# A batched double residual product: x of the first eight units loaded by four rows in a run and multiplied in 32x128 tiles

## The chip, the cores and the metric

One core of one Trainium2 chip. The metric is the time on the device in microseconds for one execution of the whole kernel; lower is better.

## The reference

For each of 128 batches b there is an x of 64 channels by 512 times (fp32), a number `itok_B_0_7[b]` that picks one of 8 matrices W0 (64x64), and a number `itok_B_1_198[b]` that picks one of 200 matrices W1 (64x64):

```python
def layer(x, index, weights):                 # einsum 'bct,bcd->bdt'
    return jnp.einsum('bct,bcd->bdt', x, weights[index])

x = x + layer(x, itok_B_0_7, L0_cond_weights)
x = x + layer(x, itok_B_1_198, L1_cond_weights)
return x
```

So out[b] = M[b]^T x[b] with M[b] = (I + W0[b]) (I + W1[b]), a 64x64 matrix for each batch. x is 16.78 MB, the output as much.

## The kernel before

**Tiling.** A slot is 4 batches, a unit two slots (8 batches, 1 MB of x). x of a slot lies in SBUF as 128 partitions: 4 batches times 32 pairs of rows; a partition holds 2 consecutive channels (J = 2) of 512 times, so each of the 128 pieces of a load is 4 KB (`x_view`, L70, L127). The array `xy` has a place for all 32 slots, and the output of a slot is written over its x. Stores have the same form (`out_view`, L72).

**Start.** SP loads the condition numbers, x of unit 0 and half of unit 1 (L129 to L131), waits for `s_w0b_early`, and then issues all the other loads. POOL makes the identity and issues the indirect DMA that gathers the 128 matrices W1 (L148). PE turns W0 by transposes (L171), DVE writes I + W0 to `w0t` (L349), and copies the 16 matrices of units 0 and 1 to `w0b` (L360); POOL copies those of units 2 to 15 (L163). Meanwhile ACT and PE work on dummy copies and transposes (L378, L176). When the gather has landed, DVE adds one to the diagonals of W1 (L365), PE transposes W1 four columns at a time (64 transposes, L186), and DVE and ACT take turns at copying them to `w1` (L269).

**M.** `products(k)` (L190) makes the M of a block of units, for each batch and each j a product of a 64x32 stationary slice of `w0b` and the 64x64 `w1`, 32 matmuls for two units. The blocks are unit 0, unit 1, and then pairs of units. DVE (even slots) and ACT (odd slots) copy M to `m_diag` (`copy_m`, L284, two operations of 128x256 for a block of two units), multiplied by a mask of zeros and ones, so that a 64x128 stationary tile holds the M of two batches with zeros beside them.

**Apply.** `apply(k)` (L211): a slot takes 2 (j) x 2 (half h of the partitions) matmuls of a 64x128 tile with 512 columns; the two halves are two row tiles and write to two PSUM banks. Each fp32 matmul is two instructions in the profile. Unit 0 alone goes by `apply_single` (L231): 32x64 tiles, eight of them side by side, with no zeros multiplied, and its M copied plainly (L276); its output is stored in 2 KB pieces (L312). DVE and ACT each copy half of a slot's output from PSUM (L303; L282 for unit 0), two operations of 64x512 for a slot and engine. ACT issues the stores, a unit at a time behind the first copy of the next unit, the last unit's two slots one by one (L305, L380).

**Order of the work.** PE: products(0), then for each block k products(k+1) and apply(k). PSUM: three pairs of banks for outputs (`Y_RING`), so that slot s waits for the copies of slot s-3, and one pair (banks 6, 7) for M. DVE and ACT: the copies in the order of PE's work.

Of the kernel before, what the change touches and what calls it, by code (L numbers as in the profile page):

```python
# [5 lines left out]
def bass_cond_residual_kernel(  # L6
# [23 lines left out]

    fp32 = mybir.dt.float32
    i32 = mybir.dt.int32
    ALU = mybir.AluOpType
# [4 lines left out]
    J = 2  # L38
    Q = C // J
    SLOT = 4  # L40
    SLOTS = B // SLOT
    UNIT = 2 * SLOT
    UNITS = B // UNIT
    BANK = 512
# [6 lines left out]
    M_COLUMNS = 4  # L51
    M_RING = 8

    M_BANKS = [6, 4] + [6] * 7
    Y_RING = 3
    TURN = 4
    TURNS = C // TURN
    W1_RING = 6

    EARLY = 2  # L60
# [7 lines left out]
    QUARTERS = [slice(r * Q, (r + 1) * Q) for r in range(SLOT)]  # L68

    x_view = x_dram.rearrange("(s b) (p j) t -> (b p) s (j t)", b=SLOT, j=J)  # L70
    single_out_view = out_dram.rearrange("(s r) c t -> s c r t", r=SLOT)
    out_view = out_dram.rearrange("(s b) (q i) t -> (b q) s (i t)", b=SLOT, i=J)  # L72

    ctx = ExitStack()
    with ctx:  # L75
# [6 lines left out]
        xy = sb("xy", [P, SLOTS, J * T], fp32)  # L82
        w0_rows = sb("w0_rows", [P, ROWS, C], fp32)
        w0t = sb("w0t", [P, S0 * C], fp32)
        w1_rows = sb("w1_rows", [B, C, C], fp32)
        w1 = sb("w1", [P, UNITS * SLOT, C], fp32)
        w0b = sb("w0b", [P, UNITS * SLOT, C], fp32)
        m_diag = sb("m_diag", [P, 2, M_RING, J, P], fp32)
        ident = sb("ident", [P, P], fp32)
        mask = sb("mask", [P, 2], fp32)  # L90
# [10 lines left out]
        s_mask = sem("s_mask")  # L101
# [4 lines left out]
        s_w0t = sem("s_w0t")  # L106
        s_w1_plus = sem("s_w1_plus")
# [15 lines left out]

        @block.sync
        def _(sp):
            def load(s, n):
                sp.dma_start(xy[:, s:s + n, :], x_view[:, s:s + n, :]).then_inc(s_x[s // 2], 16)  # L127

            sp.dma_start(cond[:, :], cond_dram.rearrange("(b o) -> b o", o=1)).then_inc(s_cond, 16)  # L129
            load(0, 2)  # L130
            load(2, 1)  # L131

            sp.wait_ge(s_w0b_early, EARLY * UNIT)
            load(3, 1)
            for v in range(2, UNITS):
                load(2 * v, 2)
            for v in range(UNITS):
                sp.wait_ge(s_out[v], 32 if v < SINGLE or v == UNITS - 1 else 16)

        @block.gpsimd  # L140
        def _(pool):
# [12 lines left out]
            for first in range(EARLY * UNIT, B, 2 * UNIT):  # L154
                _, picked = nc.values_load_multi_w_load_instructions(  # L155
                    subjects[0:1, first:first + 2 * UNIT], engines=(POOL,), min_val=0, max_val=S0 - 1,
                    skip_runtime_bounds_check_because="subjects index the 8 matrices")
                if first == EARLY * UNIT:
                    pool.wait_ge(s_gather, 16)
                    pool.wait_ge(s_w0t, 4)  # L160
                for n in range(2 * UNIT):
                    v, odd, r = (first + n) // UNIT, n // SLOT % 2, n % SLOT
                    nc.gpsimd.tensor_copy(w0b[HALVES[odd], v * SLOT + r, :],  # L163
                                          w0t[HALVES[odd], bass.ds(picked[n] * C, C)]).then_inc(s_w0b, 1)

        @block.tensor
        def _(pe):
# [21 lines left out]

            def products(k):  # L190

                first, n = BLOCKS[k]
                if first + n <= EARLY:
                    pe.wait_ge(s_w0b_early, UNIT * (first + n))
                else:
                    pe.wait_ge(s_w0b, UNIT * (first + n - EARLY))
                if k >= 2:

                    pe.wait_ge(s_m_v, 2 * k)
                    pe.wait_ge(s_m_s, 2 * k)  # L200
                for v in range(first, first + n):
                    for j in range(J):
                        for r in range(SLOT):
                            for odd, rows in enumerate(HALVES):
                                at = (v % M_COLUMNS * J + j) * C
                                last = nc.tensor.matmul(psum[QUARTERS[r], M_BANKS[k] + odd, at:at + C],  # L206
                                                        w0b[rows, v * SLOT + r, j * Q:(j + 1) * Q],
                                                        w1[rows, v * SLOT + r, :], start=True, stop=True)
                last.then_inc(s_m_psum, 1)

            def apply(k):  # L211

                first, n = BLOCKS[k]
                pe.wait_ge(s_m_v, 2 * (k + 1))
                pe.wait_ge(s_m_s, 2 * (k + 1))
                for s in range(2 * first, 2 * (first + n)):
                    v, odd = s // 2, s % 2
                    pe.wait_ge(s_x[v], 32 if v == 1 else 16)
                    if s >= Y_RING:

                        pe.wait_ge(s_y_v, 2 * (s - Y_RING + 1))
                        pe.wait_ge(s_y_s, 2 * (s - Y_RING + 1))
                    for j in range(J):
                        for h, rows in enumerate(HALVES):
                            last = nc.tensor.matmul(psum[:, 2 * (s % Y_RING) + h, :],  # L225
                                                    m_diag[rows, odd, v % M_RING, j, :],
                                                    xy[rows, s, j * T:(j + 1) * T],
                                                    start=j == 0, stop=j == J - 1)
                    last.then_inc(s_y_psum, 1)

            def apply_single(k):  # L231

                v = BLOCKS[k][0]
                pe.wait_ge(s_m_v, 2 * (k + 1))
                pe.wait_ge(s_m_s, 2 * (k + 1))
                pe.wait_ge(s_x[v], 32 if v == 1 else 16)
                for half in range(2):
                    s = 2 * v + half
                    if s >= Y_RING:

                        pe.wait_ge(s_y_v, 2 * (s - Y_RING + 1))
                        pe.wait_ge(s_y_s, 2 * (s - Y_RING + 1))
                    for j in range(J):
                        for h in range(2):
                            rows = QUARTERS[2 * half + h]
                            for odd, columns in enumerate(HALVES):
                                last = nc.tensor.matmul(psum[columns, 2 * (s % Y_RING) + h, :],  # L247
                                                        m_diag[rows, odd, v, j, 0:C],
                                                        xy[rows, 2 * v + odd, j * T:(j + 1) * T],
                                                        start=j == 0, stop=j == J - 1)  # L250
                    last.then_inc(s_y_psum, 1)
# [4 lines left out]
            for k in range(len(BLOCKS)):  # L256
                if k + 1 < len(BLOCKS):
                    products(k + 1)
# [149 lines left out]
```

## Time and profile before

| | |
|---|---|
| median of 3 runs | 92.74 us (92.63 to 92.84) |
| the profiled execution's own time | 92.7 us |
| its span, first to last instruction | 90.8 us |
| granted TensorE clock, mean over the span | 0.968 |
| busy: PE, DVE, ACT, POOL | 76.8, 60.0, 57.0, 23.5 us |
| DMA | 35.93 MB, mean 396 GB/s |

Times in the rows are microseconds from the start of the span. In the timelines and the chain, L12 is line 12 of the kernel, PE a matmul, PEld a weight load, "q" behind an engine its sequencer, where DMAs are issued. "x32" counts instructions.

### The profile page before, as it was taken

What the parts mean: (1) busy time and instruction counts of PE and PEld (TensorE: products, weight loads), DVE (VectorE), ACT (ScalarE), POOL (GpSimd) and SP (SyncE); (2) the same over time, 40 slices, a digit from 0 to 9 for tenths busy, and PEclk for the clock granted to TensorE, in tenths of its full rate; (3) what the DMA queues carried; (4) which work ended last, traced back from release to release, by engine and by line L of the source; (5) the groups of instructions that cost most, each with busy time, mean ns of one, the idle gap of its engine ahead of it and who ended that gap; (6) DMA issues with size and microseconds to landing.
All of it is one profiled execution on the core that took longest, in us unless ns stands there. A gap on an engine that the chain in (4) does not pass through costs nothing.

```text
span 90.8 us, 2458 instructions
## 1 busy us (share of the span) xinstructions
PE 76.8 (85%) x906; PEld 42.9 (47%) x906; DVE 60.0 (66%) x124; ACT 57.0 (63%) x114; POOL 23.5 (26%) x119
## 2 busy tenths in 40 slices
PE   0599959977999999999999999999999999992000
PEld 0489749965545443544544454454444444440000
DVE  1096019994388787978878788888787887887000
ACT  2899807885367675867776677777576775775000
POOL 3400049989998988000000000000000000000000
PEclk9999999999999999999999999999999999999755
DMA  0999999999999999999999999999999999999992
GB/s 6 337 446 424 455 361 415 420 399 409 409 413 402 409 418 394 419 418 424 411 415 426 415 413 420 420 422 420 411 415 422 420 419 428 404 424 420 419 399 103
DMA packets 9453, 35.93 MB, mean 396 GB/s; under 512 B 737, under 2 KB 866, under 8 KB 9314
## 3 DMA queue, kind: packets, MB, share of 16 engines
q1 hardware_dynamic: 4512, 16.78, 46.1%
q10 hardware_dynamic: 4786, 16.91, 45.8%
q0 software_dynamic: 144, 2.10, 5.4%
q8 instruction: 7, 0.11, 0.5%
q14 instruction: 4, 0.03, 0.1%
HBM read 19.01 MB, written 16.78 MB: 394 GB/s over the span
## 4 chain that ended last, share of the span: by engine, by line
PE 68%; DMA 12%; DVE 9%; issue 1%; DVEq 1%; ACTq 0%; POOLq 0%
PE psum L225 58%; DMA w_rows<-in_L_cond_weights_dram,cond 10%; DVE w L269 7%; PE psum L206 7%; PE psum L247 2%; DMA subjects<-in_itok_B_dram 2%; DVEq L75 1%; PE psum L186 1%; DVE xy L303 1%; ACTq L370 0%; DVE m_diag L276 0%; DVE w_rows L365 0%; POOLq L155 0%; DVEq L275 0%
## 5 line engine op out<-in xcount | busy, mean ns | idle before, releaser
L225 PE MATMUL psum<-xy,m_diag 64*128 64x512 f32 x240 | 53.4, 595 | 0.0
L303 DVE COPY xy<-psum 64x512 f32<-64x512 f32 x60 | 41.0, 684 | 11.1 <-PE psum L225 10.2
L303 ACT COPY xy<-psum 64x512 f32<-64x512 f32 x60 | 34.9, 582 | 17.5 <-PE psum L225 16.8
L225 PEld LDWEIGHTS psum<-xy,m_diag 64*128 64x128 f32 x240 | 22.6, 187 | 25.6 <-issue 25.0
L163 POOL COPY w0b<-w0t 64x64 f32 x112 | 21.7, 237 | 10.1 <-DMA w_rows<-in_L_cond_weights_dram,cond 8.2
L206 PEld LDWEIGHTS psum<-w,w0b 64*32 64x32 f32 x512 | 5.6, 105 | 6.4 <-issue 3.0
L269 ACT COPY w<-psum 64x256 f32<-64x256 f32 x16 | 5.8, 365 | 3.8 <-PE psum L186 2.8
L186 PE MATMUL psum<-ident,w_rows 128*64 128x128 f32 x64 | 7.2, 274 | 1.0 <-DVE w_rows L365 1.0
L378 ACT COPY w<-w_rows 128x256 f32<-128x256 f32 x18 | 7.3, 405 | 0.8 <-DMA w_rows<-in_L_cond_weights_dram 0.2
L186 PEld LDWEIGHTS psum<-ident,w_rows 128*64 128x64 f32 x64 | 7.0, 151 | 1.3 <-DVE w_rows L365 1.3
L206 PE MATMUL psum<-w,w0b 64*32 64x64 f32 x512 | 6.9, 224 | 0.9 <-DVE w L269 0.9
L269 DVE COPY w<-psum 64x256 f32<-64x256 f32 x16 | 6.7, 417 | 1.2 <-PE psum L186 0.8
L176 PE MATMUL psum<-ident,w_rows 128*64 128x128 f32 x54 | 7.5, 303 | 0.0
L176 PEld LDWEIGHTS psum<-ident,w_rows 128*64 128x64 f32 x54 | 6.5, 126 | 1.0 <-ACT w L378 0.4
L295 DVE TENSOR_SCALAR m_diag<-psum,mask 128x256 f32<-128x256 f32 (+1 forms) x16 | 6.7, 462 | 0.2
L295 ACT ACTIVATE m_diag<-psum,mask 128x256 f32<-128x256 f32 (+1 forms) x16 | 6.5, 460 | 0.2
L171 PE MATMUL psum<-ident,w_rows 128*64 128x128 f32 x4 | 1.0, 414 | 3.4 <-DMA w_rows<-in_L_cond_weights_dram 3.4
L349 DVE TENSOR_TENSOR w0t<-psum,ident 64x256 f32<-64x256 f32 x4 | 1.5, 412 | 3.3 <-PE psum L171 3.3
L365 DVE TENSOR_SCALAR w_rows<-w_rows 128x64 f32<-128x64 f32 x1 | 0.2, 225 | 4.0 <-DMA w_rows<-in_L_cond_weights_dram,cond 4.0
L282 DVE COPY xy<-psum 128x512 f32<-128x512 f32 x2 | 1.3, 686 | 1.8 <-PE psum L247 1.8
L378 ACT ACT_TABLE_LOAD x1 | 1.3, 1283 | 1.8 <-issue 1.8
L360 DVE COPY w0b<-w0t 64x64 f32 x16 | 2.1, 188 | 0.2
(14 smaller groups left out, 7.2 us busy)
## 6 DMA issues: line engine op xcount, KB each, us to landing
xy<-in_x_dram SPq DMA_DIRECT2D x15, 1024.0 KB, 19.7
out_dram<-xy ACTq DMA_DIRECT2D x14, 1024.0 KB, 14.4
out_dram<-xy ACTq DMA_DIRECT2D x4, 512.0 KB, 8.3
xy<-in_x_dram SPq DMA_DIRECT2D x2, 512.0 KB, 5.8
w_rows<-in_L_cond_weights_dram ACTq DMA_DIRECT2D x1, 128.0 KB, 2.5
cond<-in_itok_B_dram SPq DMA_DIRECT2D x1, 0.5 KB, 2.2
subjects<-in_itok_B_dram ACTq DMA_DIRECT2D x1, 0.5 KB
w_rows<-in_L_cond_weights_dram,cond POOLq DMA_INDIRECT x1, 9.2
```

The costliest lines, as they stand in the source:

```text
L163: nc.gpsimd.tensor_copy(w0b[HALVES[odd], v * SLOT + r, :], w0t[HALVES[odd], bass.ds(picked[n] * C, C)]).then_inc(s_w0b, 1)
L176: nc.tensor.transpose(psum[0:C, z, 0:P], w0_rows[:, z, :], ident[:, :])
L186: last = nc.tensor.transpose(psum[0:C, n % W1_RING, z * B:(z + 1) * B], w1_rows[:, :, n * TURN + z], ident[:, :])
L206: last = nc.tensor.matmul(psum[QUARTERS[r], M_BANKS[k] + odd, at:at + C], w0b[rows, v * SLOT + r, j * Q:(j + 1) * Q], w1[rows, v * SLOT + ...
L225: last = nc.tensor.matmul(psum[:, 2 * (s % Y_RING) + h, :], m_diag[rows, odd, v % M_RING, j, :], xy[rows, s, j * T:(j + 1) * T], start=j = ...
L247: last = nc.tensor.matmul(psum[columns, 2 * (s % Y_RING) + h, :], m_diag[rows, odd, v, j, 0:C], xy[rows, 2 * v + odd, j * T:(j + 1) * T], ...
L269: copy(w1[rows, :, n * TURN:(n + 1) * TURN].rearrange("q (v r) k -> q v r k", r=SLOT), turned[:, odd, :, :, :]).then_inc(done, 1)
L295: scale(to[:, b, :, :, :], psum[:, M_BANKS[k] + odd, at:at + n * J * C].rearrange("q (w e i) -> q w i e", i=J, e=Q), mask[:, b:b + 1]).the ...
L303: copy(xy[rows, s, i * T:(i + 1) * T], psum[HALVES[i], 2 * (s % Y_RING) + h, :]).then_inc(done, 1)
L349: nc.vector.tensor_tensor(w0t[rows, :].rearrange("q (s j k y) -> q j s k y", s=S0, j=J, y=J)[:, j, :, :, :], turned[:, j, :, :, :], one[:, ...
L360: nc.vector.tensor_copy(w0b[HALVES[odd], v * SLOT + r, :], w0t[HALVES[odd], bass.ds(picked[n] * C, C)]).then_inc(s_w0b_early, 1)
L378: nc.scalar.copy(w1[:, 0:ROWS, :], w0_rows[:, :, :]).then_inc(s_tick, 1)
```

## The change

The first eight units (`TWO = 8`) are "four" units: J is 4, Q is 16. A unit's x is loaded as 8 batches times 16 groups of four consecutive rows, 8 KB for each partition; unit 1 is still loaded in two parts (rows 0 and 1, then 2 and 3 of each group, 4 KB pieces). Units 8 to 15 are loaded as before. x now lies one unit's place beyond its output, so that the output of a slot is written where the x of the unit before it was.

In a four unit, 32 partitions hold two batches (16 groups each). `products(k)` multiplies for each j, each pair r of batches and each half a 64x32 slice (16 rows of the one batch's W0, 16 of the other's) by the 64x128 pair of `w1`: again 32 matmuls for two units, with 128 columns instead of 64, of which half is used; `copy_m` takes the used parts by a mask. `apply(v, half, j)` multiplies two 32x128 tiles by 512 columns; for one unit there are 2 (half) x 4 (j) x 2 (h) matmuls. They are staggered: the half 1 of step j-1 is issued behind the half 0 of step j, and the last step of half 1 behind the first of the next unit.

No unit goes by single batches any more: `apply_single`, `copy_m_single`, `copy_y_single` and the stores in 2 KB pieces are gone. All blocks are two units. `products(k+1)` is issued ahead of the second unit of block k. Even units are in partitions 0 to 63 of `w0b` and `w1`, odd ones in 64 to 127, and DVE copies the M of even units, ACT that of odd ones. PSUM is one ring of four pairs of banks that outputs and M take in the order of `USES`. DVE makes two forms of I + W0: `w0t` for the four units by two operations of 64x512, and, behind the 16 copies for units 0 and 1, `w0t_two` by four operations for the others. `mask_four` is made by one reduction of the identity.

The core of the diff:

```diff
-    BLOCKS = [(0, 1), (1, 1)] + [(v, 2) for v in range(2, UNITS, 2)]
-    SINGLE = 1
-    M_BANKS = [6, 4] + [6] * 7
-    Y_RING = 3
+    J = 4
+    I = 2
+    BLOCK = 2
+    TWO = 4 * BLOCK
+    TWOS = 4
+    USES = [("m", 0)]
+    for k in range(BLOCKS):
+        USES += [("y", 4 * k), ("y", 4 * k + 1)]
+        if k + 1 < BLOCKS:
+            USES += [("m", k + 1)]
+        USES += [("y", 4 * k + 2), ("y", 4 * k + 3)]
...
-    x_view = x_dram.rearrange("(s b) (p j) t -> (b p) s (j t)", b=SLOT, j=J)
+    x_view = x_dram.rearrange("(v b) (p j) t -> (b p) v (j t)", b=UNIT, j=J)
+    two_x_view = x_dram.rearrange("(s r) (p i) t -> (r p) s (i t)", r=PAIRS, i=I)
...
-            load(0, 2)
-            load(2, 1)
-            sp.wait_ge(s_w0b_early, EARLY * UNIT)
-            load(3, 1)
+            load_rows(0, 0, J)
+            load_rows(1, 0, 2)
+            sp.wait_ge(s_w0b_early, BLOCK * UNIT)
+            load_rows(1, 2, 2)
             for v in range(2, UNITS):
-                load(2 * v, 2)
+                if is_four(v):
+                    load_rows(v, 0, J)
+                else:
+                    load_slots(2 * v, 2)
...
+                    for j in range(J):
+                        for r in range(PAIRS):
+                            for odd, rows in enumerate(HALVES):
+                                at = (r * J + j) * 2 * Q
+                                n = k * UNIT + 2 * r
+                                last = nc.tensor.matmul(psum[QUARTERS[r], bank("m", k) + odd, j * P:(j + 1) * P],
+                                                        w0b[rows, k, at:at + 2 * Q],
+                                                        w1[rows, n:n + 2, :].rearrange("q b e -> q (b e)"),
+                                                        start=True, stop=True)
...
+            def apply(v, half, j):
+                n = 2 * v + half
+                if j == 0:
+                    wait_for_banks("y", n)
+                for h in range(2):
+                    rows = QUARTERS[2 * half + h]
+                    last = nc.tensor.matmul(psum[:, bank("y", n) + h, :], m_diag[rows, v % M_RING, j, :],
+                                            xy[rows, 2 * v + 2 + j // 2, j % 2 * T:(j % 2 + 1) * T],
+                                            start=j == 0, stop=j == J - 1)
...
             products(0)
+            for v in range(UNITS):
+                if v % BLOCK == 1 and v < UNITS - 1:
+                    products(v // BLOCK + 1)
+                wait_for_m(v)
+                pe.wait_ge(s_x[v], 32 if v == 1 else 16)
+                if v >= TWO:
+                    apply_two(v, 0)
+                    apply_two(v, 1)
+                    continue
+                for j in range(J):
+                    apply(v, 0, j)
+                    if j > 0:
+                        apply(v, 1, j - 1)
+                    elif v > 0:
+                        apply(v - 1, 1, J - 1)
+                if v + 1 == TWO:
+                    apply(v, 1, J - 1)
...
-            copy(m_diag[:, odd, v, :, 0:C], psum[:, M_BANKS[k] + odd, v * J * C:(v + 1) * J * C].rearrange(
-                "q (j e) -> q j e", j=J)).then_inc(done, 2)
...
+            if is_four(v):
+                mask = mask_four
+                made = [psum[:, bank("m", k) + odd, :].rearrange("q (j b e i) -> q b j i e", j=J, b=2, i=I)[:, b, :, :, :]
+                        for b in range(2)]
...
             for rows in HALVES:
-                for j in range(J):
+                nc.vector.tensor_tensor(
+                    w0t[rows, :].rearrange("q (s j k) -> q j s k", s=S0, j=J),
+                    w0_psum.rearrange("q (j s k) -> q j s k", j=J, s=S0),
+                    ident[0:C, 0:C].rearrange("q (o k j) -> q j o k", o=1, j=J).to_broadcast((C, J, S0, Q)),
+                    ALU.add).then_inc(s_w0t, 1)
```

## Rows read from the trace of the kernel before

**Rows 1.** the page's part 1, and the DMA line of part 2

```profile
PE 76.8 (85%) x906; PEld 42.9 (47%) x906; DVE 60.0 (66%) x124; ACT 57.0 (63%) x114; POOL 23.5 (26%) x119
...
DMA  0999999999999999999999999999999999999992
```

**Rows 2.** windows: stretch, us, busy PE PEld DVE ACT POOL, clock, DMA share, GB/s

```profile
40.00:64.00 24.00, 24.00 (x294) 11.32 (x292) 19.31 (x31) 16.55 (x31) 0.00 (x0) 1.00 1.03 418
...
82.00:88.00 6.00, 0.28 (x2) 0.00 (x0) 1.37 (x3) 1.16 (x2) 0.00 (x0) 0.75 1.02 419
88.00:89.00 1.00, 0.00 (x0) 0.00 (x0) 0.00 (x0) 0.00 (x0) 0.00 (x0) 0.50 0.72 295
```

**Rows 3.** the chain of waits in order of time: start us, us, what

```profile
3.26 9.16 DMA w_rows<-in_L_cond_weights_dram,cond
...
21.50 0.30 DVE m_diag L276
...
21.85 2.01 PE psum L247 x32
23.86 0.79 PE psum L206 x48
24.64 3.63 PE psum L225 x16
...
29.07 7.07 PE psum L225 x32
36.13 0.79 PE psum L206 x53
...
82.32 0.68 DVE xy L303
```

**Rows 4.** the page's part 3, the DMA queues

```profile
q1 hardware_dynamic: 4512, 16.78, 46.1%
q10 hardware_dynamic: 4786, 16.91, 45.8%
q0 software_dynamic: 144, 2.10, 5.4%
```

**Rows 5.** timeline of ACT at 76 to 91 us: start us, us, what

```profile
80.67 0.38 ACTq L315 DMA_DIRECT2D out_dram<-xy  x1
```

**Rows 6.** DMA issues at 80 to 82 us, and landing time

```profile
out_dram<-xy ACTq DMA_DIRECT2D x1, 1024.0 KB, 7.2
```

**Rows 7.** DMA issues at 1.0 to 1.5 us, and landing time

```profile
xy<-in_x_dram SPq DMA_DIRECT2D x1, 1024.0 KB, 5.1
...
cond<-in_itok_B_dram SPq DMA_DIRECT2D x1, 0.5 KB, 2.2
```

**Rows 8.** timeline of all engines, 20.5 to 28.3 us

```profile
20.83 0.85 PE L206 MATMUL psum<-w,w0b 64*32 64x64 f32 x64 [0.89 <-DVE w L269]
...
21.84 0.27 PEld L247 LDWEIGHTS psum<-xy,m_diag 32*64 32x64 f32 x16 [0.33 <-DVE m_diag L276]
...
22.33 0.22 PEld L247 LDWEIGHTS psum<-xy,m_diag 32*64 32x64 f32 x8 [0.21 <-issue]
22.76 0.22 PEld L247 LDWEIGHTS psum<-xy,m_diag 32*64 32x64 f32 x8 [0.21 <-issue]
...
25.29 0.87 DVE L295 TENSOR_SCALAR m_diag<-psum,mask 128x256 f32<-128x256 f32 x2
```

**Rows 9.** timeline of DVE, 0 to 13 us

```profile
4.57 1.53 DVE L349 TENSOR_TENSOR w0t<-psum,ident 64x256 f32<-64x256 f32 x4 [3.27 <-PE psum L171]
6.24 2.22 DVE L360 COPY w0b<-w0t 64x64 f32 x16
12.44 0.23 DVE L365 TENSOR_SCALAR w_rows<-w_rows 128x64 f32<-128x64 f32 x1 [3.98 <-DMA w_rows<-in_L_cond_weights_dram,cond]
```

**Rows 10.** groups by line and form: count, busy us and mean ns

```profile
L303 DVE COPY xy<-psum 64x512 f32<-64x512 f32 x60 | 41.0, 684 | 11.1 <-PE psum L225 10.2
...
L163 POOL COPY w0b<-w0t 64x64 f32 x112 | 21.7, 237 | 10.1 <-DMA w_rows<-in_L_cond_weights_dram,cond 8.2 <-issue 0.4
```

More of the change, by code:

```diff
@@ L197, in products @@
[L197 to L201, printed above, removed]
+                if k == 0:
+                    pe.wait_ge(s_w0b_early, BLOCK * UNIT)
+                else:
+                    pe.wait_ge(s_w0b, k * BLOCK * UNIT)
+                wait_for_banks("m", k)
+                if not is_four(BLOCK * k):
+                    for o in range(2):
+                        for j in range(I):
+                            for r in range(PAIRS):
+                                for odd, rows in enumerate(HALVES):
+                                    at = (o * I + j) * C
+                                    n = PAIRS * o + r
+                                    last = nc.tensor.matmul(psum[QUARTERS[r], bank("m", k) + odd, at:at + C],
+                                                            w0b[rows, k, n * C + j * H:n * C + (j + 1) * H],
+                                                            w1[rows, k * UNIT + n, :], start=True, stop=True)
+                else:
@@ L202, in products @@
                     for j in range(J):
-                        for r in range(SLOT):
+                        for r in range(PAIRS):
                             for odd, rows in enumerate(HALVES):
[L205 to L208, printed above, removed]
@@ L209, in products @@
-                last.then_inc(s_m_psum, 1)
[L211 to L222, printed above, removed]
-                    for j in range(J):
[L224 to L228, printed above, removed]
-                    last.then_inc(s_y_psum, 1)
@@ L231, in apply_single @@
[L231 to L251, printed above, removed]
+                                at = (r * J + j) * 2 * Q
@@ new lines, in apply_two @@
+            def apply_two(v, half):
+                n = 2 * v + half
+                wait_for_banks("y", n)
+                for i in range(I):
+                    for h, rows in enumerate(HALVES):
+                        last = nc.tensor.matmul(psum[:, bank("y", n) + h, :], m_diag[rows, v % M_RING, I * half + i, :],
+                                                xy[rows, n + 2, i * T:(i + 1) * T],
+                                                start=i == 0, stop=i == I - 1)
+                last.then_inc(s_y_psum, 1)
@@ new lines, in _ @@
+            _, picked = nc.values_load_multi_w_load_instructions(
+                subjects[0:1, 0:BLOCK * UNIT], engines=(DVE,), min_val=0, max_val=S0 - 1,
+                skip_runtime_bounds_check_because="subjects index the 8 matrices")
+            dve.wait_ge(s_w0t, 2)
+            for n in range(BLOCK * UNIT):
+                put_w0(nc.vector, s_w0b_early, picked[n], n // UNIT, n % UNIT)
+            for rows in HALVES:
+                for i in range(I):
+                    nc.vector.tensor_tensor(
+                        w0t_two[rows, :].rearrange("q (s i k y) -> q i s k y", s=S0, i=I, y=2)[:, i, :, :, :],
+                        w0_psum.rearrange("q (y i s k) -> q i s k y", y=2, i=I, s=S0)[:, i, :, :, :],
+                        ident[0:C, 0:C].rearrange("q (o k y i) -> q i o k y", o=1, y=2, i=I)[:, i, :, :, :]
+                        .to_broadcast((C, S0, Q, 2)), ALU.add).then_inc(s_w0t_two, 1)
```

182 lines of the change are left out of this document (87 added, 95 removed).

## The prediction

> **What bounds the kernel now.** I read the busy times and the DMA line first [rows 1], then the windows [rows 2], the chain [rows 3] and the last stores [rows 5, 6]. PE is busy 85% of the span, and the DMA line is at 9 in every slice but the first and the last. The windows say the same more exactly: from 40 to 64 us the DMA share is 1.03 at 418 GB/s with PE busy all 24.00 us, and from 82 to 88 us, when PE has 0.28 us of work left, the DMA still moves 419 GB/s; only in 88 to 89 does it fall to 0.72 [rows 2]. So the 35.93 MB are moved without a gap, and DMA ends the kernel. The chain goes through PE, though: it is followed back by semaphores and knows no queue of bytes. It shows PE without a gap from 21.85 us to the first copy of the last slot at 82.32 [rows 3], in a period of 7.07 + 0.79 = 7.86 us for two units.
>
> Two clocks therefore run side by side, and the question is how far PE may slip before its end becomes the kernel's. The store of unit 14 (1 MB) is issued at 80.67 and lands 7.2 us later, at 87.9 [rows 5, 6]; the last unit's MB follows at about 2.5 us (1.05 MB at 419 GB/s), to 90.4, and the span closes at 90.8. What would that store take with nothing queued ahead? Two rows of the empty start bound it: the first load of 1 MB lands after 5.1 us, sharing the DMA with 0.13 MB of W0 (0.3 us), so 4.8; a DMA of 0.5 KB in 128 pieces lands after 2.2 us [rows 7], and 1.05 MB add 2.5, which makes 4.7, with the handling of 128 tiny pieces in it. From below, the 2.5 us of bytes and some 1.7 us of latency give 4.2. I take 4.5. **The slack is 7.2 - 4.5 = 2.7 us** (2.1 to 3.0): a shift of PE's end up to that costs nothing, and what lies beyond it counts in full.
>
> **What the change gives to DMA.** Pieces of 4 KB: 46.1% of 16 engines for 90.8 us, over 4096 pieces, is 163.5 ns each. Pieces of 16 KB (the gather, 5.4%, 128 pieces): 613 ns, or 153.2 for 4 KB [rows 4]. If a piece costs x for each 4 KB and c once, x + c = 163.5 and x + c/4 = 153.2, so c = 13.7 ns. Seven units lose 128 pieces each (256 of 4 KB become 128 of 8 KB; unit 1, in two parts, keeps its 256): 896 x 13.7 / 16 = 0.77 us. Unit 0's output is stored in 256 pieces of 4 KB instead of 512 of 2 KB: 0.22 us. Together 1.0 us less DMA work, from below 0 if the 10 ns are not a price of the piece, and no reason to be more. It is worth something only while DMA bounds.
>
> **What it costs PE, part by part.**
> 1. The gather is awaited at the start (DVE idle 3.98 us until 12.44 [rows 9]), behind 1.5 MB of x of which 1 MB now comes in 8 KB pieces: 128 fewer, -0.1 us.
> 2. The two 64x512 additions instead of four of 64x256 (1.53 us [rows 9]), the 16 copies with a pattern of 4x16 (2.22 us), the mask's reduction and `w0t_two` (four operations again, 1.5 us) are DVE's work before 12.44 us; 8.46 + 1.5 = 10.0, so they are covered with over 2 us to spare. SP's wait for `s_w0b_early` goes with the 16 copies; what is queued behind it, the loads, meets a DMA that is busy with the gather until 12.4 [rows 3]: nothing, up to 2 us of lateness. The 64 transposes and the copies of W1 keep their sizes: nothing, +-0.3 for the new order of runs. POOL's copies take 237 ns each [rows 10]: 16 for a block in 3.8 us of the 7.86; even at twice the price they hold.
> 3. First M. Now 32 instructions for unit 0 alone are started at 20.83, and DVE begins its copy at 21.50 [rows 8, 3]. Then all of block 0 is made first: 64 instructions of 128 columns. Two units take 16 rounds for their 7.07 us [rows 3], so 512 columns are 0.44 us and 128 columns 0.11; eight tiles (two halves of the rows, four quarters of the columns) get eight instructions each, 0.88 us, against four rounds of 64 columns, 0.22. That is +0.65. The copy is two masked operations, 0.87 [rows 8], instead of 0.30 [rows 3]: +0.57. PE's first apply moves from 21.85 to 23.1: **+1.2**.
> 4. Unit 0 goes from 2.01 us to the time of the others, 3.53: **+1.5**. For the seven other four units I take the same 3.53: 16 matmuls of four row tiles instead of 8 of two. The row for it is unit 0 now: its 32 instructions are of 32 rows, and the loads come 8 in 0.43 us (22.33, 22.76 [rows 8]), so four quarters of the rows, with two column tiles each, work side by side in 2.01 us.
> 5. Products. The 0.79 us ahead of a block's applies [rows 3] hold 64 instructions of 64 columns, where the tiles alone need 8 x 0.055 = 0.44; with 128 columns they need 0.88. The increase lies between 0 and 0.44 for blocks 1 to 3; I take 0.15 each, as most of the issuing hides behind the columns: **+0.45**.
> 6. The stagger. Half 1 of a unit is one step (0.86 us) behind half 0. At the first `products` half 0 has done four steps and half 1 three, and it stays one behind until unit 7: 33 steps instead of 32, each end half empty. If PE changes from one tile shape to another only when all tiles are done, this is **+0.86**; if the products can start in the idle half, down to 0.
> 7. PSUM and copies. An output now takes 2 x 684 ns on DVE [rows 10], M 0.87 for two units: 4 x 1.37 + 0.87 = 6.4 us in a block of 7.9. y(2v) and y(2v+1) end one step apart instead of two, but the third bank pair behind is free 1.4 us after its output, before it is wanted again: nothing, with about 0.4 us of cover, and up to +1 over the four blocks if a copy is late.
>
> The Trainium skill ("TensorEngine Tiling (Array Packing)", section Tiling Modes) says that a change of the tiling mode drains TensorE. The rows cannot show it, since the tiles end together there; by it term 6 is the full step, without it nothing.
>
> Sum: -0.1 + 1.2 + 1.5 + 0.45 + 0.86 = 3.9, rounded with term 7's small risk to 4.0. PE ends at 86.3 instead of 82.3. Less the slack, 4.0 - 2.7 = +1.3. The profiled execution took 92.7 us, its span 90.8, and the median is 92.74, so the same number serves: 92.7 + 1.3 = **94.0 us**. The DMA is idle for moments near the end, and its 1.0 us is lost in that.
>
> **The rivals.**
> A. PE slips less than the slack, DMA stays the bound and its saving is what one sees. This needs the half step (0.86) to vanish and the first M to be cheaper, so that the shift is 2.5 or less; by terms 3 and 4, 2.7 us alone, that is not easy, but slack up to 3.0 helps. Time: 92.7 - 1.0 = 91.7 to 92.5. For it: DMA's 1.03 share to 88 us [rows 2]. This is the other side: it decides at a PE end of 84.5.
> B. The two meet: shift 2.6 to 3.0, time within 0.2% (92.55 to 92.93; about what a measurement can tell from no change).
> C. Copies become the bound in the four units: DVE has 1.5 us of spare time in a block; if the waits for the ring of banks eat it, each of four blocks loses 0.3 to 0.7 us: 95.2 to 96.8. Against it: today DVE waits for PE at nearly every output, 10.2 us in sum [rows 10].
> D. Row tiles do not overlap as I say. If matmuls started strictly in program order, the two instructions of one 32-row matmul would have to follow one another on the same tile, and only two tiles would work at once: eight units at 6.9 instead of 3.5 us, some 27 us more, about 121 us. The rows speak against it: 16 weight loads at once at 21.84, half of them for rows that come 16 instructions later in the program [rows 8]. The Trainium skill ("TensorE: Matmul & The Clock Gate", section Part 3: Packing small matmuls) states this order, strict first in first out; here the row disagrees.
>
> **Chances.** Forecast (93.2 to 95.1) 0.66, A 0.17, B 0.10, C 0.05, D 0.02. Faster 0.17, same 0.10, slower 0.73. The range, 92.0 to 95.1, takes in the forecast's case with its bounds (shift 3.2 to 5.1), B, and the upper half of A; D, C and the lower part of A are left out.
>
> **What would show it.** Right: first 32-row matmul near 23.1 us; 3.4 to 3.5 us for a four unit; PE's end near 86.3; DMA share under 1 somewhere between 83 and 87 us; the store of unit 14 landing in about 5 us instead of 7.2; mean duration of the loads' pieces per byte down by 4%. Wrong: PE's end before 84.5 with the last store still landing 6 to 7 us after its issue (A); idle PE with DVE as releaser (C); weight loads in twos instead of fours (D).

## The result, and the profile after

The changed kernel takes 95.68 us (median of 5 runs, 95.51 to 95.89) against 92.67 us (5 runs, 92.61 to 92.84): a ratio of 1.032, 95% interval 1.030 to 1.034, slower by 3.0 us. The direction was forecast, the size was not: 94.0 us, range 92.0 to 95.1. The profiled execution took 95.89 us with a span of 94.0 (before: 92.7 and 90.8). Here and below a run's time is the median of all its executions, while the ratios leave out those in the chip's slower state, over 1.5% above the fastest of the same kernel.

From the page of the kernel after, parts 1 to 3 in extract:

```profile
PE 82.2 (87%) x1018; PEld 46.4 (49%) x1018; DVE 64.0 (68%) x128; ACT 58.4 (62%) x115; POOL 22.8 (24%) x119
...
DMA  0999999999999999999999999999999998569695
...
q10 hardware_dynamic: 4514, 16.91, 44.5%
q1 hardware_dynamic: 3616, 16.78, 44.3%
```

The DMA line is no longer at 9 to the end, as it was in [rows 1]: from slice 34 on it has gaps. The loads' queue has 896 pieces fewer than in [rows 4], as the diff says. The windows of the kernel after (stretch, us, busy PE, PEld, DVE, ACT, POOL, clock, DMA share, GB/s):

```profile
40.00:64.00 24.00, 24.00 (x356) 11.35 (x350) 19.60 (x32) 16.82 (x31) 0.00 (x0) 1.00 1.03 418
72.00:80.00 8.00, 8.00 (x100) 3.85 (x98) 6.34 (x10) 5.50 (x10) 0.00 (x0) 1.00 0.94 379
80.00:88.00 8.00, 8.00 (x40) 3.51 (x38) 6.53 (x10) 5.72 (x10) 0.00 (x0) 1.00 0.68 272
```

From 80 to 88 us PE has all of its time filled and the DMA 0.68 of its own, where the kernel before had a DMA share of 1.02 in 82 to 88 [rows 2]. PE is the bound now. Its way there stands in the chain of waits of the kernel after, in order of time (start us, us, what):

```profile
3.31 10.10 DMA w_rows<-in_L_cond_weights_dram,cond
...
21.82 1.18 PE psum L266 x63
...
23.12 0.89 DVE m_diag L347 x2
...
24.05 3.70 PE psum L284 x28
27.75 1.09 PE psum L266 x64
28.84 7.21 PE psum L284 x64
36.05 1.09 PE psum L266 x64
...
52.65 0.79 PE psum L256 x53
53.44 4.50 PE psum L284 x36
57.94 3.63 PE psum L296 x16
...
88.62 0.68 DVE xy L353
```

L266 are the products of 128 columns, L284 the 32x128 tiles, L256 and L296 products and applies of units 8 to 15. Against [rows 3]: the gather ends at 13.41 instead of 12.42; PE's first apply starts at 24.05 instead of 21.85; a product phase of the four units takes 1.09 instead of 0.79 us, a pair of them 7.21 instead of 7.07; PE ends at 88.6 instead of 82.3. The last stores, in the timeline of ACT (first row) and the DMA issues of 86.5 to 87.5 us:

```profile
86.97 0.38 ACTq L359 DMA_DIRECT2D out_dram<-xy  x1
...
out_dram<-xy ACTq DMA_DIRECT2D x1, 1024.0 KB, 4.0
```

Unit 14's store now lands 4.0 us after its issue, not 7.2 [rows 5, 6]: nothing is queued ahead of it.

### The profile page after: what moved, and what is told of

It is laid out like the page before. It is cut to its first block, busy times and chain, and to the rows that moved or that the text cites. A ratio compares the mean times of both kernels' runs of the same rounds, so it can differ in the third digit from the quotient of the medians.

```text
span 94.0 us, 2693 instructions
## 1 busy us (share of the span) xinstructions
PE 82.2 (87%) x1018; PEld 46.4 (49%) x1018; DVE 64.0 (68%) x128; ACT 58.4 (62%) x115; POOL 22.8 (24%) x119
## 3 DMA queue, kind: packets, MB, share of 16 engines
q1 hardware_dynamic: 3616, 16.78, 44.3%
## 4 chain that ended last, share of the span: by engine, by line
PE 71%; DMA 13%; DVE 9%; issue 1%; DVEq 1%
PE psum L284 32%; PE psum L296 30%; DMA w_rows<-in_L_cond_weights_dram,cond 11%; DVE w L327 7%; PE psum L266 5%; PE psum L256 3%; DMA cond<-in_itok_B_dram 2%; DVE m_diag L347 1%; DVEq L85 1%; DVE xy L353 1%; PE psum L229 1%; DVE w_rows L415 0%; DVEq L332 0%
## 5 line engine op out<-in xcount | busy, mean ns | idle before, releaser
L353 DVE COPY xy<-psum 64x512 f32<-64x512 f32 x64 | 43.7, 683 | 15.9 <-PE psum L284 9.8
L284 PE MATMUL psum<-xy,m_diag 32*128 32x512 f32 x256 | 30.1, 601 | 1.1 <-DVE m_diag L347 1.1
L296 PE MATMUL psum<-xy,m_diag 64*128 64x512 f32 x128 | 28.6, 596 | 0.0
L284 PEld LDWEIGHTS psum<-xy,m_diag 32*128 32x128 f32 x256 | 13.1, 184 | 15.0 <-issue 11.2
L296 PEld LDWEIGHTS psum<-xy,m_diag 64*128 64x128 f32 x128 | 12.1, 187 | 14.2 <-issue 13.9
L175 POOL COPY w0b<-w0t_two 64x64 f32 x64 | 11.9, 240 | 0.9 <-issue 0.4
L178 POOL COPY w0b<-w0t 64x64 f32 x48 | 9.0, 243 | 9.8 <-DMA w_rows<-in_L_cond_weights_dram,cond 9.2
L266 PE MATMUL psum<-w,w0b 64*32 64x128 f32 x256 | 4.6, 273 | 0.9 <-DVE w L327 0.9
L266 PEld LDWEIGHTS psum<-w,w0b 64*32 64x32 f32 x256 | 3.6, 105 | 3.4 <-POOL w0b L175 1.5
L347 DVE TENSOR_SCALAR m_diag<-psum,mask_four 128x256 f32<-128x256 f32 x8 | 3.5, 478 | 1.7 <-PE psum L266 1.6
L256 PEld LDWEIGHTS psum<-w,w0b 64*32 64x32 f32 x256 | 2.8, 105 | 3.0 <-issue 3.0
L347 ACT ACTIVATE m_diag<-psum,mask_four 128x256 f32<-128x256 f32 x8 | 3.4, 470 | 1.5 <-PE psum L266 1.4
```

What stands on the lines that cost most here:

```text
L175: eng.tensor_copy(w0b[rows, v // 2, n * C:(n + 1) * C], w0t_two[rows, bass.ds(picked * C, C)]).then_inc(done, 1)
L178: eng.tensor_copy(w0b[rows, v // 2, :].rearrange("q (r j b p) -> q r b j p", r=PAIRS, j=J, b=2) [:, n // 2, n % 2, :, :], w0t[rows, bass.d ...
L256: last = nc.tensor.matmul(psum[QUARTERS[r], bank("m", k) + odd, at:at + C], w0b[rows, k, n * C + j * H:n * C + (j + 1) * H], w1[rows, k * ...
L266: last = nc.tensor.matmul(psum[QUARTERS[r], bank("m", k) + odd, j * P:(j + 1) * P], w0b[rows, k, at:at + 2 * Q], w1[rows, n:n + 2, :].rear ...
L284: last = nc.tensor.matmul(psum[:, bank("y", n) + h, :], m_diag[rows, v % M_RING, j, :], xy[rows, 2 * v + 2 + j // 2, j % 2 * T:(j % 2 + 1) ...
L296: last = nc.tensor.matmul(psum[:, bank("y", n) + h, :], m_diag[rows, v % M_RING, I * half + i, :], xy[rows, n + 2, i * T:(i + 1) * T], sta ...
```

## The experiments

The times of the kernel before beside these runs were 92.67 to 92.77 us; ratios are to it.

**Moving PE's end alone (e2, e3).** Into the kernel before, ahead of `products(0)`; 4 pairs in e2, 7 in e3:

```diff
+            for n in range(4):
+                for h, rows in enumerate(HALVES):
+                    nc.tensor.matmul(psum[:, 6 + h, :], ident[rows, :],
+                                     w1_rows[rows, 0:8, :].rearrange("q d e -> q (d e)"), start=True, stop=True)
             products(0)
```

> The kernel before, with 4 pairs of dummy 64x128 matmuls of 512 columns ahead of the first products: PE is about 3.5 us late from there to its end (82.3 becomes about 85.7) and nothing else is changed. Slack theory (a store of 1 MB lands 7.2 us after its issue in the kernel before and 4.05 us in the changed kernel, so PE may slip by 7.2 - 4.05 = 3.15 us for nothing): +0.3 to +0.5 us, 93.0 to 93.2. My slack of the prediction, 2.7 us: +0.8, 93.5. Rival (PE alone ends the kernel, no slack): +3.5, 96.2.

> The same with 7 pairs, about 6.05 us late, nearly the slip of the changed kernel (6.3 us). Slack of 3.15 us: +2.9 us, 95.6, and a DMA share under 1 in the last 15 us as in the changed kernel. Slack of 2.7: +3.35, 96.0. If the changed kernel's loss came from something other than PE's late end, this one would not reach its 95.7.

Measured: e2 93.94 us, ratio 1.011 (1.006 to 1.015); e3 96.54, ratio 1.044 (1.039 to 1.048). The single times of each scatter by over 1 us, and PE's end is known in the profiled executions alone (93.73 us in e2; 95.91 us in e3, the fastest of its four), so the reading goes by these. PE's end moved by 4.2 us in e2 (to 86.5, the gather having landed 0.4 us later as well), its span is 91.9; in e3 it moved by 6.4, span 94.1. Last rows of e3's chain, and two of its windows:

```profile
74.70 13.96 PE psum L225 x64
88.68 0.68 DVE xy L307
```

```profile
80.00:88.00 8.00, 8.00 (x40) 3.56 (x38) 6.47 (x10) 5.67 (x10) 0.00 (x0) 1.00 0.69 277
88.00:90.00 2.00, 0.63 (x4) 0.00 (x0) 1.65 (x3) 1.31 (x3) 0.00 (x0) 1.00 1.01 401
```

This is the kernel before with its old loads, its old tiles and a late PE, and it has the changed kernel's last 15 us: PE ends at the same time (its last output is copied from 88.68 and 88.62), the DMA share is the same (0.69 and 0.68), and so is the span (94.1 and 94.0). In e2, in e3 and in the changed kernel 5.4 us lie between PE's end and the span's (91.9 - 86.5, 94.1 - 88.7, 94.0 - 88.6), against 8.5 in the kernel before. So the slack was 8.5 - 5.4 = 3.1 us, and the changed kernel's loss is PE's slip of 6.3 us less 3.1. That is a reading of single executions: by its median e3 is 3.8 us above the kernel before, 0.9 us above the changed kernel, and that difference is not explained.

**A slip inside the slack (e6).** The kernel before with `SINGLE = 0` and `copy_m` for block 0:

```diff
-    SINGLE = 1
+    SINGLE = 0
...
-            copy_m_single(eng, copy, m_done, odd, 0)
+            copy_m(eng, scale, m_done, odd, 0)
```

> The kernel before with unit 0 multiplied like the others (SINGLE = 0): M copied by the mask (0.61 instead of 0.30 us), 3.6 instead of 2.0 us for unit 0, output stored in 4 KB pieces. PE's end moves by about +1.9 us, to 84.2. Slack theory (3.1 us): no change in time, 92.6 to 92.8. Rival (every us of PE counts): 94.6. Rival (the 2 KB pieces cost: 256 pieces fewer at 7.6 ns, 0.12 us): 92.6, not to be told from no change.

Measured: 92.90 us, ratio 1.0005 (0.998 to 1.003). Two rows of its chain:

```profile
22.57 3.71 PE psum L225 x16
...
84.77 0.68 DVE xy L303
```

Unit 0 takes 3.71 us instead of 2.01, PE ends 2.45 us later than before (0.4 of it from the gather), and the time does not change: below the slack PE's microseconds are free.

**What long pieces are worth (e4).** The kernel before, units 2 to 15 loaded like this:

```diff
+    long_view = x_dram.rearrange("(v b) (p j) t -> (b p) v (j t)", b=UNIT, j=4)
...
-                load(2 * v, 2)
+                sp.dma_start(xy[:, 2 * v:2 * v + 2, :].rearrange("q s t -> q (s t)"), long_view[:, v, :]).then_inc(s_x[v], 16)
```

> The kernel before, with x of units 2 to 15 loaded in pieces of 8 KB (four rows in a run) into the same places. The multiplications are left as they are, so x's rows stand in other partitions than the products expect: only the time has a meaning. 14 x 128 = 1792 pieces fewer, DMA being the bound of this kernel. By the prediction's 13.7 ns for a piece: 1792 x 13.7 / 16 = 1.5 us less, 91.1 to 91.2. By the medians of the traces (309 ns for 8 KB, 159 for 4 KB, 9 ns a piece): 1.0 us less, 91.7. Rival (stores and loads share a limit in bytes, a piece costs nothing): 92.6 to 92.7.

Measured: 91.90 us, ratio 0.991 (0.989 to 0.993), 0.85 us less for 1792 pieces, which is 0.85 x 16 / 1792 = 7.6 ns for a piece. The saving is real, where DMA bounds; at that price the changed kernel's 896 pieces are worth 0.43 us. A second reading is the loads' queue in part 3 of e4's page, its share times 16 engines times the span of 90.0 us:

```profile
q1 hardware_dynamic: 2720, 16.78, 45.2%
```

That is 651 us of engine time against 670 in the kernel before [rows 4], or 10.5 ns for a piece saved. In the changed kernel itself the same sum gives 666 us (44.3% of 16 x 94.0): 4 us less for 896 pieces, half of what e4's price would give.

**The stagger (e5).** The changed kernel with

```diff
                 for j in range(J):
                     apply(v, 0, j)
-                    if j > 0:
-                        apply(v, 1, j - 1)
-                    elif v > 0:
-                        apply(v - 1, 1, J - 1)
-                if v + 1 == TWO:
-                    apply(v, 1, J - 1)
+                    apply(v, 1, j)
```

> The changed kernel without the stagger: in each four unit the half 1 of step j is issued right behind the half 0 of step j, 32 steps instead of 33. Step theory: the half-empty step of 0.86 us goes (unit 7's 4.50 us in the chain becomes 3.6), and so do the 0.14 us by which a pair of units waits for M (7.21 against 7.07, three times); but both outputs of a unit now end together, so the second output of every odd unit must wait until the first output of the unit before is copied (two copies of 0.69 us, 1.45 us, against products of 1.09 us): 0.4 us for each of four blocks. PE's end 88.6 - 0.86 - 0.42 + 1.5 = 88.8, time 95.6 to 96.0 if the gather lands at 13.4 as before. Rival (the stagger costs nothing, since the tiles catch up): unit 7 stays at 4.5 us or PE's end moves later by the whole 1.5 us, 97.

Measured: 95.80 us, ratio 1.030 (1.024 to 1.037), the changed kernel's time. Rows of its chain:

```profile
23.85 3.71 PE psum L284 x32
27.56 1.09 PE psum L266 x64
28.65 7.54 PE psum L284 x62
...
37.27 7.09 PE psum L284 x64
...
53.76 3.96 PE psum L284 x32
...
88.40 0.68 DVE xy L348
```

Unit 7 falls from 4.50 to 3.96 us, as the step theory says in sign though not in full, and two of the pairs rise to 7.5. From the first apply to PE's end it is 88.38 - 23.85 = 64.53 us, in the changed kernel 88.60 - 24.05 = 64.55. The stagger neither costs nor saves on balance: without it unit 7 takes 0.54 us less and the third pair 0.12 less, and the two other pairs take 0.33 more each, which is as much; there weight loads wait twice for DVE's copies of outputs, 0.3 us in sum.

**The late gather (e1, e7, e8, e9, e10).** The changed kernel's gather landed 1.0 us later, which the prediction had not seen. e1 (the changed kernel with the half of unit 1 taken by batches):

```diff
-            load_rows(1, 0, 2)
+            sp.dma_start(x_of(1)[0:C, :], x_view[0:C, 1, :]).then_inc(s_x[1], 16)
...
-            load_rows(1, 2, 2)
+            sp.dma_start(x_of(1)[C:P, :], x_view[C:P, 1, :]).then_inc(s_x[1], 16)
```

> The changed kernel, except that unit 1's x is loaded in two parts by batches (four batches, 64 partitions of 8 KB each) and no longer by rows (rows 0 and 1 of every group of four, 128 pieces of 4 KB, 8 KB apart). In the changed kernel's trace the gather of W1 lands at 13.41 us instead of 12.42. Theory G (the strided 4 KB pieces of that half unit are slow and hold the gather up): the gather lands near 12.4, PE's first apply starts near 23.1 instead of 24.05, and the time falls from 95.7 to about 94.7. Theory H (it is the 8 KB pieces of unit 0 in front, the longer additions on DVE, or chance): the gather stays at 13.2 to 13.5 and the time at 95.6 to 95.8.

Measured: 101.05 us, ratio 1.084 (1.078 to 1.090); both theories missed. The gather landed at 16.3 us. PE's dummy work had ended 4.8 us before its first transpose of W1, and the clock granted to it fell; windows of e1:

```profile
12.00:16.00 4.00, 0.00 (x0) 0.00 (x0) 0.00 (x0) 0.00 (x0) 0.00 (x0) 0.73 1.00 274
16.00:20.00 4.00, 3.36 (x16) 2.85 (x17) 1.56 (x5) 0.73 (x2) 3.32 (x18) 0.50 0.98 397
```

The DMA is busy (1.00) and moves only 274 GB/s. The loads' queue of e1 from 6 to 7 us, while the second early load is under way:

```profile
q1 hardware_dynamic: 33, 0.26, 117.7%
```

33 pieces of 8 KB for 1.177 x 16 engines' microseconds are 571 ns each; two pieces of 4 KB in the kernel before take 327 on the mean [rows 4]. In the same stretch of the changed kernel 74 pieces of 4 KB fill 100.1% of the 16 engines, 216 ns each or 433 for 8 KB, so a part of the slowness was there already. What e1 added changes several things at once (64 partitions as destination instead of 128, pieces of 8 KB instead of 4, for both parts of unit 1), and no run separates them. The granted clock fell from 1.00 to 0.50 (1.2 GHz) in the stretch without work on PE, and the first transposes of W1 ran at that level.

e7 is the changed kernel with no part of unit 1 ahead of the gather:

```diff
-            load_rows(1, 0, 2)
...
-            load_rows(1, 2, 2)
+            load_rows(1, 0, J)
```

> The changed kernel with no part of unit 1 loaded ahead of the gather: unit 1 comes whole, in 8 KB pieces, behind the wait for the early copies. Theory G (the half of unit 1 in 4 KB pieces 8 KB apart stands in the gather's way, 1.25 us of bytes and about 1 us of slowness): the gather lands at 11.4 to 12.0 us instead of 13.4, PE's first apply starts at about 22.4 instead of 24.05, time about 94.1 to 94.4. If the gather's descriptors are not ready before 7 us, it lands at about 12.3 and the time is 94.6. Theory H (lateness by chance or by something else): the gather stays over 13.

Measured: 94.26, 94.57, 96.32 and 96.41 us, too far apart for a verdict. In its profile (94.57) the gather landed at 11.60 and PE ended at 86.8, 1.8 us sooner than in the changed kernel, while the span fell by 1.3 only (92.7).

e8 is the kernel before with unit 1 in strided halves, e9 the kernel before with unit 0 in 8 KB pieces, e10 has both (`long_view` as in e4). The first two lines are e9's, the others e8's, whose second half (rows 2 and 3 of each group) takes the place of `load(3, 1)`:

```diff
-            load(0, 2)
+            sp.dma_start(xy[:, 0:2, :].rearrange("q s t -> q (s t)"), long_view[:, 0, :]).then_inc(s_x[0], 16)
...
-            load(2, 1)
+            sp.dma_start(xy[:, 2, :], long_view[:, 1, 0:2 * T]).then_inc(s_x[1], 16)
```

> The kernel before, with unit 1's x loaded as in the changed kernel: first rows 0 and 1 of each group of four (4 KB pieces 8 KB apart), later rows 2 and 3. The output of unit 1 is not the reference's (its rows stand elsewhere than M expects). Theory G (the pieces 8 KB apart are slow): the gather lands at 13.2 to 13.5 us instead of 12.4 to 12.9 in the four profiles of kernels with the old load, PE's end moves by 0.5 to 1.0 and is hidden by the slack, time 92.7 to 92.9. Theory H (not the distance, but the 8 KB pieces of unit 0 or DVE's longer additions): the gather lands at 12.4 to 12.9.

> The kernel before with x of unit 0 alone loaded in 8 KB pieces (its output is then not the reference's). So far the gather of W1 lands at 12.42 to 12.88 us in six profiles with unit 0 in 4 KB pieces (one of them with the strided half of unit 1) and at 13.20 and 13.41 in two with unit 0 in 8 KB pieces and the strided half. Theory L (8 KB pieces of unit 0 in front slow down what follows them): the gather lands at 13.1 to 13.5, and the pieces between 6 and 8 us take over 200 ns for 4 KB. Theory D (DVE's longer additions, or both loads together): 12.4 to 12.9 and 159 to 170 ns. Time unchanged in both, 92.5 to 92.9, by the slack.

> The kernel before with both early loads as in the changed kernel (unit 0 in 8 KB pieces, rows 0 and 1 of unit 1 as 4 KB pieces 8 KB apart), DVE's work as before; the outputs of units 0 and 1 are not the reference's. If the loads together are the cause: gather at 13.1 to 13.5. If it is 12.4 to 12.9, the cause is in the changed kernel's engines (DVE's two additions of 64x512 instead of four of 64x256) and not in its loads.

Measured: e8 92.94 us (ratio 1.004, 1.001 to 1.006), 92.78 for a single execution of e9 and 93.21 of e10. The reading is the start of DVE's addition behind the gather. In seven profiles with unit 0 in 4 KB pieces and a part of unit 1 ahead, e8's 12.88 among them, it lies between 12.44 and 12.90. In the four with unit 0 in 8 KB pieces it lies between 13.22 (e5) and 13.55 (e10); the row of e9:

```profile
13.45 0.23 DVE L366 TENSOR_SCALAR w_rows<-w_rows 128x64 f32<-128x64 f32 x1 [4.89 <-DMA w_rows<-in_L_cond_weights_dram,cond]
```

e9 changes that one load alone, so the long pieces of unit 0 are what makes the gather late, by 0.7 us from middle to middle, and not their distance in unit 1 nor DVE's additions. Behind this stands one profile of e9; the distance of 1.0 us to the kernel before holds scatter too.

They do so only with the half of unit 1 between them and the gather. Without it the rows of e7 (unit 0 in 8 KB pieces) and of e13 (below, unit 0 in 4 KB pieces) are:

```profile
11.62 0.23 DVE L414 TENSOR_SCALAR w_rows<-w_rows 128x64 f32<-128x64 f32 x1 [1.00 <-DMA w_rows<-in_L_cond_weights_dram,cond]
...
11.82 0.22 DVE L364 TENSOR_SCALAR w_rows<-w_rows 128x64 f32<-128x64 f32 x1 [3.27 <-DMA w_rows<-in_L_cond_weights_dram,cond]
```

There the long pieces cost nothing. From 6 to 7 us the gather's queue moves 0.25 MB in the kernel before, 0.13 in e9 and nothing in the changed kernel, so what stands ahead of it is done later. How the long pieces bring that about stays open: the pieces behind them that I expected to take longer in e9 did not, and in e10 and the changed kernel they do. e9's time did not move, since 0.7 us lie in the slack.

**Keeping the saving (e11, e12, e14).** The changed kernel with units 0 and 1 in the old form, unit 0 by single batches, units 2 to 7 (e11) or 2 to 11 (e12) in the new one, and unit 1 loaded whole behind the early copies. The core of it:

```diff
-    TWO = 4 * BLOCK
+    TWO = 8
     def is_four(v):
-        return v < TWO
+        return BLOCK <= v < TWO
...
-            load_rows(0, 0, J)
-            load_rows(1, 0, 2)
+            load_slots(0, 2)
...
+                if v == 0:
+                    pe.wait_ge(s_m_v, 2)
+                    pe.wait_ge(s_x[0], 16)
+                    apply_single()
+                    continue
```

> A version meant to keep the saving in DMA and give back the slip of PE: the changed kernel with units 0 and 1 in the old form (two rows, unit 0 by single batches with its M copied first), units 2 to 7 in the new one, and unit 1 loaded whole behind the early copies. PE's end by the step theory: 82.3 of the kernel before, +0.3 (products of unit 0 in half of the rows, M copied by DVE alone), +0.9 (three products of 128 columns), +0.3 (M late twice), +0.9 (half step), +0.2 (one more change of tile shape), -1.2 (gather earlier, as in e7): 83.7, below 85.4, so DMA ends the kernel, with 768 pieces fewer at 7.6 ns / 16 = 0.36 us: 92.3. If the slack theory did not hold: 94.

> The same with units 2 to 11 in the new form: two blocks more, +0.9 us for PE, whose end comes at 84.6, just where PE and DMA meet; 1280 pieces fewer, 0.61 us: 92.1 if DMA still ends it, 92.3 if PE does. Both hybrids together: more than before by at most 0.6%, and the order of the two tells whether a block pays (0.12 us of DMA gained for 0.44 us of PE).

Measured: e11 93.91 us, ratio 1.013 (1.010 to 1.015); e12 93.97, ratio 1.013 (1.010 to 1.016). PE's end was nearly as computed (84.2 and 85.1), the time was not. The windows of e11 show the end:

```profile
88.00:89.00 1.00, 0.00 (x0) 0.00 (x0) 0.00 (x0) 0.00 (x0) 0.00 (x0) 0.77 1.00 410
89.00:90.00 1.00, 0.00 (x0) 0.00 (x0) 0.00 (x0) 0.00 (x0) 0.00 (x0) 0.50 0.58 238
90.00:91.00 1.00, 0.00 (x0) 0.00 (x0) 0.00 (x0) 0.00 (x0) 0.00 (x0) 0.50 0.18 74
91.00:92.00 1.00, 0.00 (x0) 0.00 (x0) 0.00 (x0) 0.00 (x0) 0.00 (x0) 0.50 0.06 25
```

A share of 0.18 and then 0.06 is as much as three engines of sixteen and then one would do, while the others have finished. Two more kernels separate the load from the four-row form. e13 is the kernel before with unit 1 loaded whole behind the early copies, e14 is e11 with `load_slots(2, 1)` ahead and `load_slots(3, 1)` behind:

```diff
-            load(2, 1)
...
-            load(3, 1)
+            load(2, 2)
```

> The kernel before with unit 1 loaded whole behind the early copies, as in e7 and in both hybrids, and nothing else changed. In both hybrids PE ended at 84.2 and 85.1 us, yet the span ended at 92.5 and 91.7: the last bytes came on one or two of the 16 DMA engines after the others had finished, and the first pieces of the gather took 943 to 989 ns on average instead of 612. Theory S (moving that half load lets some DMA engines fall behind, and a kernel that DMA bounds ends with the slowest): the gather lands at 11.2 to 11.7, PE ends at about 81.2, and the time nevertheless rises by 0.7 to 1.3 us, to 93.4 to 94.0. Theory F (it is the four-row form in the hybrids, not the load): 92.5 to 92.8.

> e11 with the loads of the kernel before in front of the gather (unit 0 and the first slot of unit 1 in 4 KB pieces). PE's end 84.2 + 1.0 to 1.2 = 85.2 to 85.4, which the slack just covers (5.4 us from PE's end to the span's: 90.6 to 90.8); DMA's own end is 90.8 - 0.36 = 90.4. Theory S: 92.3 to 92.7, no worse than before. Theory F: it stays at 93.7 to 94.0.

Measured: e13 94.12 us, ratio 1.014 (1.010 to 1.017); e14 92.88, ratio 1.002 (0.999 to 1.005). e13's gather landed 0.6 us sooner, PE ended 0.6 us sooner, and the kernel was 1.3 us slower. A row of its chain and three of its windows:

```profile
81.70 0.68 DVE xy L302
```

```profile
88.00:89.00 1.00, 0.00 (x0) 0.00 (x0) 0.00 (x0) 0.00 (x0) 0.00 (x0) 0.50 0.96 393
89.00:90.00 1.00, 0.00 (x0) 0.00 (x0) 0.00 (x0) 0.00 (x0) 0.00 (x0) 0.50 0.67 274
90.00:91.00 1.00, 0.00 (x0) 0.00 (x0) 0.00 (x0) 0.00 (x0) 0.00 (x0) 0.50 0.25 102
```

So the moved load alone makes a DMA-bound kernel end later, on a few engines; why these fall behind is not shown. e14, without it, is level with the kernel before: PE ended at 85.4, where the two clocks meet (85.4 + 5.4 = 90.8), so the saving of 768 pieces (0.36 us by e4's price) had nothing left to shorten. No version here that computes the whole product beats the kernel before.

## Why the prediction was right in sign and wrong in size

The two clocks, and the rule that only PE's slip beyond the slack counts, are what the runs showed (e3, e6). The sum, term by term, in us (term 2 was put at nothing and cost nothing: DVE still waited 2.78 us for the gather, and from there to the first products it is 8.4 us in both kernels):

| step of the prediction | forecast | measured |
|---|---|---|
| 1. gather | -0.1 | +1.0 |
| 3. first M (both units made first, masked copy) | +1.2 | +1.2 (24.05 - 13.43 against 21.85 - 12.44) |
| 4. unit 0 | +1.5 | +1.7 (3.70 against 2.01) |
| 5. products, three | +0.45 | +0.9 (1.09 against 0.79) |
| 6. half step | +0.86 | +1.06 (4.50 + 3.63 against 7.07) |
| 7. copies | 0.1 | +0.4 (7.21 against 7.07, three times) |
| PE's end | +4.0 | +6.3 |
| slack | -2.7 | -3.1 |
| the span | +1.3 | +3.2 |

**Term 1 failed, and is the largest miss:** 1.1 of the 2.3 us by which the forecast of PE's end fell short. I counted pieces (128 fewer, 0.1 us) for a load that stands in front of the gather, and took a transfer's place in the queue as all that matters. The runs showed +1.0 in the changed kernel, of which e9 gives some 0.7 to the 8 KB pieces of unit 0 ahead of a half of unit 1, the rest being within the scatter of the gather's landing (12.4 to 12.9 with unchanged loads). It lay open in the prediction's own chain: everything on PE before 21.85 us hangs on this landing, and it had a bound for a gain only.

**Term 5 was under-sized.** I had both ends, 0 and 0.44 for a block, and took 0.15 on the argument that issuing hides behind the columns. Measured is 0.30: the columns come on top for the most part.

**Term 7 failed in a small way.** It named the copies of outputs and a ring of banks; what came late was M. In the timeline of the kernel after:

```profile
31.41 0.88 DVE L347 TENSOR_SCALAR m_diag<-psum,mask_four 128x256 f32<-128x256 f32 x2
...
32.34 0.31 PEld L284 LDWEIGHTS psum<-xy,m_diag 32*128 32x128 f32 x8 [0.68 <-DVE m_diag L347]
```

DVE finishes M at 32.29 and the weights of the next unit's first tiles, which could have been loaded ahead, wait for it until 32.34; each of three pairs takes 0.14 us more for it. The second output of a unit, one step late by the stagger, stands ahead of M in DVE's order. In e5 that goes (7.09 in one pair), and the banks take its place.

**Term 6** was right in place and size: unit 7 takes 4.50 us, 0.87 more than 3.63. The remaining 0.19 are one further change of tile shape, at unit 8, which I had left out: in the kernel before one unit between products takes 3.63 us and two take 7.07, so a unit is 3.44 and each such stretch costs 0.19 besides. Term 4 took half of a pair and so lacked half of that 0.19. The Trainium skill ("TensorEngine Tiling (Array Packing)", Tiling Modes) says that a change of the tiling mode drains TensorE. The trace agrees, with the full step in unit 7's 4.50 us, though e5, where the halves go in step, keeps 0.3 of it (3.96 against 3.63), which is not explained.

**The slack** was 3.1, not 2.7, just beyond the range of 2.1 to 3.0 that I gave it: 1 MB lands after 4.0 us with nothing ahead, less than the 4.2 that I took as the lower bound. The 1.7 us of latency in that bound came from no row; 4.0 less 2.5 us of bytes leaves 1.5. With the measured PE end and my slack the span would have been +3.6: this error made up for 0.4 us of the others, by luck.

**The DMA saving** was bounded well (0 to 1.0) and priced too high: 7.6 to 10.5 ns a piece in e4 against 13.7, and in the changed kernel the loads' time per byte fell by 0.5% where I had named 4% as a sign. One likely reason, which no run tests: my two rows were shares of whole queues, in which the loads' pieces also pay for the first microseconds. It did not matter to the result, since DMA no longer bounds.

**The rivals.** A (DMA stays the bound) failed by PE's end, 88.6 against 84.5, and B (the two meet) with it. C (copies bound the four units) failed by the chain: the three pairs of four units take 7.21 us, 0.14 more than before, where C needed 0.3 to 0.7 a block, and what came late there was M and not a bank. That 95.7 us lies within C's price, 95.2 to 96.8, is chance. D failed, as the timeline of PE's weight loads in the kernel after shows:

```profile
29.30 0.20 PEld L284 LDWEIGHTS psum<-xy,m_diag 32*128 32x128 f32 x4 [0.22 <-issue]
29.73 0.20 PEld L284 LDWEIGHTS psum<-xy,m_diag 32*128 32x128 f32 x4 [0.22 <-issue]
30.16 0.20 PEld L284 LDWEIGHTS psum<-xy,m_diag 32*128 32x128 f32 x4 [0.22 <-issue]
```

Four loads of 32 rows stand in each round of 0.43 us, and a pair of units takes 7.21 us, not 13.8, so four row tiles do work at once. The range, up to a slip of 5.1 us, would have had to reach 6.3; what it lacked most was an upper bound for term 1.

## What to carry to other kernels

Where a chain of waits and a full DMA line both span the kernel, measure how long the last store takes with and without a queue ahead: the difference (here 7.2 - 4.0 = 3.2 us, and 3.1 by the spans) is what the chain may slip for nothing, and beyond it every microsecond counts in full. A saving in bytes or pieces is worth something only while it is not bought on the chain; here at most 0.4 us of DMA cost 6.3 us of PE. And a load that stands ahead of the transfer on which the start hangs gets a bound for a loss as well, whatever its count of pieces says.

## What the runs showed of the hardware

- Pieces of 8 KB instead of 4 KB save 7.6 ns of a DMA engine for each piece less by the kernel's time, 10.5 by the queue's (e4). The time holds the scatter of the slowest engine too, which e13 shows.
- 1 MB in 8 KB pieces ahead of a gather made the gather land 0.7 us later than the same 1 MB in 4 KB pieces (four profiles against seven, no overlap), with 0.5 MB more between them and the gather. Without that 0.5 MB there was no such difference (11.62 in e7, 11.82 in e13).
- The same 0.5 MB ahead of the gather and 0.5 MB beside it, each to 64 partitions in 8 KB pieces instead of to 128 in 4 KB pieces: the gather landed 2.9 us later (e1 against the changed kernel).
- This kernel, bound by DMA, ends with its slowest DMA engines. The same bytes in another order in the first 8 us moved that end by 1.3 us, and the last three microseconds had DMA shares of 0.67, 0.25 and 0.06 (e13).
- Four 32x128 tiles side by side keep the pace of two 64x128 tiles: a round of 512 columns takes 0.43 us of four tiles, and a pair of units 7.09 us in e5 against 7.07 before.
- After 4.8 us without work on PE the granted clock was 0.50 (1.2 GHz; e1), and from the gather to the first products it took 10.3 us (16.36 to 26.67) instead of 8.4 (12.44 to 20.83).
